# A state-space stage of four separate batches rewritten as one program with a slot for each state

## The reference, cut to what matters

```python
def _L1_attn_ref(x, W_in, conv_w, conv_b, W_x, W_dt, b_dt, A_log, D, W_out):
    xi, z = jnp.split(x @ W_in, 2, axis=-1)              # 2 x 256 channels
    xc = _silu(causal_depthwise_conv(xi, conv_w) + conv_b)   # 4 taps
    dt, Bm, Cm = jnp.split(xc @ W_x, [8, 24], axis=-1)   # 8, 16 and 16 columns
    delta = jax.nn.softplus(dt @ W_dt + b_dt)
    A = -jnp.exp(A_log)                                  # 256 x 16
    dA = jnp.exp(delta[..., None] * A)
    dBu = delta[..., None] * Bm[:, :, None, :] * xc[..., None]
    # over the 512 tokens: h = dA_t * h + dBu_t;  y_t = sum over the 16 states of h * C_t
    y = ys + xc * D
    return y * _silu(z) @ W_out
```

## Time and profile before

| | us |
|---|---|
| median of 3 runs | 3414.8 |
| lowest, highest | 3409.95, 3416.41 |
| the profiled execution's own time | 3410.95 |
| its span | 3409.0 |
| PE busy | 2794.3 (82%) |
| DVE busy | 2085.9 (61%) |
| ACT busy | 1303.8 (38%) |
| POOL busy | 913.6 (27%) |
| mean granted clock of PE | 0.907 |

### The profile page before, as it was taken

How to read it: one execution, slowest core, us unless ns; L and a number is a source line. 1 busy time by engine, 2 the same in 40 slices (tenths; PEclk the granted TensorE clock), 3 DMA queues, 4 the chain that set the end, 5 groups by cost and what they waited for, 6 DMA issues and landing times. The chain is left out here.

```text
span 3409.0 us, 40692 instructions
## 1 busy us (share of the span) xinstructions
PE 2794.3 (82%) x14561; PEld 1289.6 (38%) x14608; DVE 2085.9 (61%) x4159; ACT 1303.8 (38%) x2241; POOL 913.6 (27%) x1160
## 2 busy tenths in 40 slices
PE   4996969855565698999998999996965699698998
PEld 1332424411121353344555343443433133254555
DVE  5884861297788564566675556556667787464444
ACT  1664642233333253222121333332742466354221
POOL 2101100075467210233251545453125110110000
PEclk9997879987788798999998999997976899799999
DMA  5221300100000320121221000002200321320000
GB/s 129 36 36 48 61 22 1 50 0 0 0 1 0 64 42 2 26 51 29 63 59 43 1 1 1 1 1 38 38 0 0 54 36 25 90 45 2 1 1 13
DMA packets 45480, 94.81 MB, mean 28 GB/s; under 512 B 14168, under 2 KB 33420, under 8 KB 39520
## 3 DMA queue, kind: packets, MB, share of 16 engines
q1 hardware_dynamic: 45280, 92.22, 12.4%
HBM read 46.20 MB, written 1.38 MB: 14 GB/s over the span
## 5 line engine op out<-in xcount | busy, mean ns | idle before, releaser
L1630 POOL TENSOR_TENSOR mamba_dbu<-mamba_du,mamba_b 128x512 f32<-128x512 f32 x128 | 256.1, 2033 | 132.3 <-ACT mamba_b L1613 132.3
L1597 PE MATMUL ps<-mamba_hc,weights 128*128 128x512 f32 x256 | 164.3, 732 | 97.2 <-DVE mamba_hc L1655 96.8
L1644 DVE TENSOR_TENSOR_SCAN mamba_h<-mamba_da,mamba_dbu 128x512 f32<-128x512 f32 x128 | 211.0, 1651 | 18.3 <-ACT mamba_da L1618 18.3
L2423 DVE TENSOR_REDUCE skv_negmax<-ps 128x2 f32<-128x256 f32 (+3 forms) x128 | 105.0, 823 | 147.5 <-PE ps L2271 147.5
L534 DVE TENSOR_REDUCE L3a_negmax<-ps 128x1 f32<-128x512 f32 x256 | 162.3, 683 | 52.0 <-PE ps L294 33.7
L534 DVE TENSOR_REDUCE L0a_negmax<-ps 128x1 f32<-128x512 f32 x256 | 162.4, 683 | 50.3 <-PE ps L294 45.9
L397 ACT ACTIVATE L0a_probs<-ps 128x512 f32<-128x512 f32 x256 | 143.6, 599 | 76.6 <-PE ps L313 65.4
L397 ACT ACTIVATE L3a_probs<-ps 128x512 f32<-128x512 f32 x256 | 143.7, 599 | 74.0 <-PE ps L313 62.9
L2485 ACT ACTIVATE skv_probs<-ps 128x1024 f32<-128x1024 f32 (+3 forms) x128 | 90.2, 704 | 205.3 <-PE ps L2297 205.3
L164 POOL TENSOR_SCALAR vareps<-mv 128x4 f32<-128x4 f32 x24 | 7.6, 315 | 547.6 <-DVE mv L1271 493.4
L1801 PE MATMUL ps<-stream,xT 128*128 128x512 f32 x256 | 132.9, 640 | 10.7 <-DVE moa_v L2054 6.5
(11 more groups left out here) (625 smaller groups left out, 6661.0 us busy)
## 6 DMA issues: line engine op xcount, KB each, us to landing
moa_masks<-picked SPq DMA_DIRECT2D x32, 512.0 KB, 6.7
stream<-stream SPq DMA_DIRECT2D x32, 192.0 KB
stream<-gate_up_down_in SPq DMA_DIRECT2D x1, 4352.0 KB, 13.4
stream<-value_output_in SPq DMA_DIRECT2D x1, 4096.0 KB, 12.3
moa_gateb<-gates SPq DMA_DIRECT2D x32, 128.0 KB
stream<-ffn_in SPq DMA_DIRECT2D x1, 2888.0 KB, 9.3
L0a_qs<-L0a_qs SPq DMA_DIRECT2D x16, 128.0 KB
L0x_qs<-L0x_qs SPq DMA_DIRECT2D x16, 128.0 KB
```

Of the source, the lines that this page charges most:

```text
L1597: pe.matmul(ps[:, 4 + j, :], k.ident, hc[:, (J * n + j) % RING, :], start=n == 0, stop=n == N - 1).then_inc(s["summed"], 1)
L1630: pool.tensor_tensor(dbu[:, i % RING, :], du[:, j, :], bsb[:, n % AHEAD, :], ALU.mult).then_inc(s["dbu_ready"], 1)
L1644: dve.tensor_tensor_scan(out=hs[:, i % RING, :], data0=da[:, i % RING, :], data1=dbu[:, i % RING, :], initial=0.0, op0=ALU.mult, op1=ALU.a ...
L2423: dve.tensor_reduce(negmax[:, g % 4, qt, at:at + 2], ps[:, bank:bank + 2, 0:(qt + 1) * P], AX.X, ALU.max, negate=True).then_inc(s["maxed"], 1)
```

## The change

`mamba(k)` is called once and is one phase over the four batches. Time is counted in slots: slot S of every engine's program holds state S mod 16 of batch S div 16 (64 slots with scans, S = 0 to 63), and behind it, in the same slot, the extra steps whose turn it is. A step "at" A for batch b stands in slot 16 b + A, so the preparation of batch b, at -12 to -4, stands in slots 4 to 12 of the batch before, and the outputs, at 16 to 20, in slots 0 to 4 of the batch after. For the first batch the preparation stands in slots with no scans.

Steps of the preparation, with the slot (batch 0's count) on each engine: projection of xi, PE -12; copy, ACT -11; convolution, PE -11, as four matmuls a half with diagonal matrices of the taps, made once by POOL; silu, ACT -10; projection to step rows and B/C rows, PE -10; copies, ACT -9; step sizes, PE -9; their bias, ACT -8; split of B/C, now on POOL, -8; z, PE -8, silu of z, ACT -7; lower part, DVE -8; exp and plus one, now both on ACT, -7; rounding, DVE -6; ln, ACT -5; sum, DVE -5; delta and du, now on POOL, -4. Outputs: DVE 16, PE 17; residual and statistics, DVE 18; inverse deviation, POOL 19; rescale, DVE 19; transposes, PE 19; copy, ACT 20.

xc, sz, delta, du and bc have two buffers. The rings of scans and weighed units lie in the `stream` tile, so the load of `stream` moves behind the stage, into a block of its own. B has one PSUM bank, C three, two banks hold the sums and two serve the extra steps. After each product POOL waits for its own semaphore.

The core of the diff:

```diff
-def mamba(k, next_stream):
+def mamba(k):
...
+    TAPS, RING, C_RING, B_RING, LEAD = 4, 6, 3, 3, 2
...
+    B_BANK, C_BANK, SUM_BANK, P_BANK, Q_BANK = 0, 1, 4, 6, 7
+    XI_AT, CONV_AT, XD_AT, DT_AT, Z_AT, LOW_AT, U_AT, ERR_AT, LN_AT, DELTA_AT = -12, -11, -10, -9, -8, -8, -7, -6, -5, -4
+    Y_AT, OUT_AT, RESID_AT, XT_AT = 16, 17, 18, 19
+    FIRST, LAST = XI_AT, (BATCH - 1) * N + XT_AT + 2
...
+        hs, hc = (k.stream[:, n * RING * SEQ:(n + 1) * RING * SEQ].rearrange("p (r t) -> p r t", r=RING) for n in range(2))
...
+                def spread(i):
+                    b, n = i // N, i % N
+                    if n == 0:
+                        pe.wait_ge(s["bc_parts"], b + 1)
+                    for c, bank in ((0, B_BANK), (1, C_BANK + i % C_RING)):
+                        if c == 0 and i >= 1:
+                            pe.wait_ge(s["b_sb"], i)
+                        if c == 1 and i >= C_RING:
+                            pe.wait_ge(s["hc_ready"], J * (i - C_RING + 1))
+                        pe.matmul(ps[:, bank, :], wb(k, "stacked", ROWS3)[:, c * N + n:c * N + n + 1].to_broadcast([ROWS3, P]),
+                                  bc[:, b % 2, :], start=True, stop=True).then_inc(s["c_ready" if c else "b_ready"], 1)
...
+                def convolve(b):
+                    if b == 0:
+                        pe.wait_ge(s["taps_ready"], J * TAPS)
+                        pe.wait_ge(s["padded"], 1)
+                    for j, bank in enumerate((P_BANK, Q_BANK)):
+                        pe.wait_ge(s["xi_sb"], J * b + j + 1)
+                        take(bank, "xc_sb", J * b + j + 1)
+                        for t in range(TAPS):
+                            last = pe.matmul(ps[:, bank, :], taps[:, j, t, :], xi[:, j, t:t + SEQ], start=t == 0,
+                                             stop=t == TAPS - 1)
+                        last.then_inc(s["conv_ready"], 1)
...
+                for S in range(FIRST, LAST):
+                    if 0 <= S + LEAD < ALL:
+                        spread(S + LEAD)
+                    if 0 <= S < ALL:
+                        sums(S)
+                    if batch_at(S, OUT_AT) is not None:
+                        project_out(batch_at(S, OUT_AT))
...
+                    if batch_at(S, CONV_AT) is not None:
+                        convolve(batch_at(S, CONV_AT))
...
+                def exponential(b):
+                    act.wait_ge(s["low_ready"], b + 1)
+                    act.activation(u[:, :, :], low[:, :, :], ACT.Exp).then_inc(s["u_ready"], 1)
+                    act.wait_ge(s["u_ready"], b + 1)
+                    act.activation(w1[:, :, :], u[:, :, :], ACT.Identity, bias=1.0).then_inc(s["w1_ready"], 1)
...
+                for S in range(FIRST, LAST):
+                    if 0 <= S < ALL:
+                        copy_b(S)
+                        decay(S)
+                    if batch_at(S, CONV_AT) is not None:
+                        copy_xi(batch_at(S, CONV_AT))
+                    if batch_at(S, XD_AT) is not None:
+                        silu_conv(batch_at(S, XD_AT))
+                    if batch_at(S, DT_AT) is not None:
+                        copy_bc(batch_at(S, DT_AT))
+                    if batch_at(S, DT_AT + 1) is not None:
+                        add_dt_bias(batch_at(S, DT_AT + 1))
+                    if batch_at(S, Z_AT + 1) is not None:
+                        silu_z(batch_at(S, Z_AT + 1))
+                    if batch_at(S, U_AT) is not None:
+                        exponential(batch_at(S, U_AT))
+                    if batch_at(S, LN_AT) is not None:
+                        logarithm(batch_at(S, LN_AT))
+                    if batch_at(S, XT_AT + 1) is not None:
+                        keep_turned(k, act, s, batch_at(S, XT_AT + 1), Q_BANK)
...
+                def split_bc(b):
+                    pool.wait_ge(s["bc_sb"], b + 1)
...
+                    chain(pool.tensor_copy(out, full[:, :]))
+                    chain(pool.tensor_tensor(full[:, :], full[:, :], out, ALU.subtract))
+                    chain(pool.tensor_copy(bc[32:64, b % 2, :], full[32:64, :]))
+                    chain(pool.tensor_copy(bc[64:ROWS3, b % 2, :], full[64:ROWS3, :]))
+                    pool.tensor_tensor(bc[64:ROWS3, b % 2, :], full[64:ROWS3, :], bc[64:ROWS3, b % 2, :], ALU.subtract
+                                       ).then_inc(s["bc_parts"], 1)
...
+                def step_sizes(b):
+                    pool.wait_ge(s["v_ready"], b + 1)
...
+                    chain(pool.tensor_tensor(delta[:, b % 2], vv[:, :, :], low[:, :, :], ALU.subtract))
+                    pool.tensor_tensor(du[:, b % 2], delta[:, b % 2], xc[:, b % 2], ALU.mult).then_inc(s["du_ready"], 1)
...
+                        pool.tensor_tensor(dbu[:, m % RING, :], du[:, b % 2, j, :], bsb[:, i % B_RING, :], ALU.mult
                                            ).then_inc(s["dbu_ready"], 1)
+                        pool.wait_ge(s["dbu_ready"], m + 1)
...
-        each(lambda b: mamba(k, first(b, wstr1)))
+        mamba(k)
+        with nc.Block() as block:
+            @block.sync
+            def _(sp):
+                stream_in(sp, wstr1)
         cross_attention(k, "L1x", R8, masks=(m1q, m1k, ALU.is_equal))
```

More of the change, by code:

```diff
@@ L1600, in _, with take @@
[L1600 to L1605 removed]
+                reader = {P_BANK: None, Q_BANK: None}
+                def take(bank, sem, n):
+                    if reader[bank]:
+                        pe.wait_ge(*reader[bank])
+                    reader[bank] = (s[sem], n)
@@ new lines, in project_bc @@
+                def project_bc(b):
+                    pe.wait_ge(s["xc_sb"], J * (b + 1))
+                    take(P_BANK, "xd_sb", b + 1)
+                    for j in range(J):
+                        last = pe.matmul(ps[0:R, P_BANK, :], w_x[:, j, 0:R], xc[:, b % 2, j, :], start=j == 0, stop=j == J - 1)
+                    last.then_inc(s["xd_ready"], 1)
+                    take(Q_BANK, "bc_sb", b + 1)
+                    for j in range(J):
+                        last = pe.matmul(ps[0:ROWS3, Q_BANK, :], w_x[:, j, R:R + ROWS3], xc[:, b % 2, j, :], start=j == 0,
+                                         stop=j == J - 1)
+                    last.then_inc(s["bc_ready"], 1)
@@ new lines, in project_out, with turn_x @@
+                def project_out(b):
+                    pe.wait_ge(s["y_in"], b + 1)
+                    take(P_BANK, "y_read", b + 1)
+                    for t in range(NT):
+                        for j in range(J):
+                            last = pe.matmul(ps[:, P_BANK, t * D:(t + 1) * D], y[:, j, t * P:(t + 1) * P], w_out[:, j, :],
+                                             start=j == 0, stop=j == J - 1)
+                    last.then_inc(s["y_ready"], 1)
+                def turn_x(b):
+                    take(Q_BANK, "xT_sb", b + 1)
+                    turn_tokens(k, pe, s, b, Q_BANK)
@@ L3169, in each @@
                 stage(b)
-        def first(b, src):
-            return lambda sp: stream_in(sp, src) if b == 0 else None
         R8 = DH ** -0.5
```

372 lines of the change are left out of this document (199 added, 173 removed).

## The result

The changed kernel took 3474.7 us in the median (3473.1 to 3479.1) beside 3412.4 for the kernel before on the same chip (3408.0 to 3416.4): ratio 1.0185 [1.0167, 1.0203], 1.9% slower, +62 us. Forecast was 3430, range 3385 to 3465: the right side and, as will be shown, the right mechanism in the main, but +17 where +62 came, and 10 us outside the range. The profiled execution took 3474.5 us around a span of 3472.4.

A forecast was written before the change was run, and what follows sets the result against it. Stage: VectorE's scans taking turns with POOL's product, one per 2.15 us, bound it. 33.5 + 276.4 + 3 × (43.0 + 8.0) + 12.7 + 0.6 + 3.4 = 479.6 against 462.6, +17.0: forecast 3430 us, range 3385 to 3465.

The forecast's parts named there:

- hidden after all: Rival: ACT's copy of b is not held by the extra steps; 14.3 us a batch, 3320 us; chance 0.08.
- The slack of 2.8 us: Time b has to spare after its copy on ACT and POOL's 1.26 us, the only cover for the extra steps.
- POOL becomes the bound: Rival at POOL's queue, slots 11 and 12: own waits 10 us, delta and du 4.4 each; 22 more, 3452; chance 0.08.
- Part (c): Preparations of batches 1 to 3 inside the slots: each extra step stalls the scans, 43.0 us per batch.
- results, slots 1 to 5: Outputs of the last batch: VectorE 1.41 + 1.22, residual 1.94, rescale with transposes 2.7; 7.3 us.
- sharing a turn: Scans on VectorE after POOL's runs: two later go at 1.72 a pair, neighbouring stalls share a turn; 3.3 us off.
- part d: PE's clock: 46 passes in the seven chains, partly at half clock; 8 us a batch, bounds 0 to 19.7.
- PE cold throughout: Rival: all 46 PE passes at half clock, 19.7 us a batch; 35 more, 3465 us; chance 0.12.
- (b): First preparation, nothing beside it, convolution on PE: first scan at 33.5 us against 30.95.
- (e): Last tail 12.7 us and stage end 0.6, as now.
- (f): Load of `stream` in its own block delays L1x's start: +2.6 + 0.8 = 3.4 us.
- The two sets of tables: ACT loads separate tables for exp and ln; one set for both would cost 3 us less in all, 3427.

The follow-up runs named there:

- The two runs with the scan first: Changed kernel, POOL's second product waits for the first half's scan: states 1 to 10 and 13, 3469.2 us; then states 6 to 9 of three batches, 3461.1 us.
- The last experiment: Inverse deviation and rescale one slot later, on the version with b and decays ahead, convolution in two slots and POOL's bursts halved: 3364.2 us, ratio 0.9863.
- The filling run: Changed kernel with zero-matrix matmuls added before a state's second sum on PE, 4, or 12 in most stalling slots: 3449.8 us, ratio 1.0106.
- POOL's halved steps: Split of B/C in two slots, delta and du in two, on the version with b and decays ahead and convolution in two slots (3376.6 us): 3376.3 us.
- the run with the load alone: Kernel before, with only the load of `stream` moved behind the stage into its own block: 3416.0 us beside 3409.9, ratio 1.0010.

## Why the prediction was right in its mechanism and short in its sizes

**What held.** That ACT's in-order queue holds b and the decays of the state after next behind each extra step: moving those alone gave back 92 us, and running the steps apart, with that order kept, 91. Which slots stall: 5 to 9, 11 and 12, each one behind the slot of its step, while 10 and 13 to 15 do not, and the longest behind the convolution. The price of an unstalled slot: POOL's wait for itself costs nothing (4.29 us a slot, and 4.29 before in most slots of the same measure). Delta and du on POOL at 2.34 us each (2.45 estimated). ln and the step sizes, 2.8 and 6.9 over a normal slot (2.7 and 6.6). The rival *hidden after all* fell: the slack of 2.8 us was no match for chains of 5 to 13. Neither price of *POOL becomes the bound* came: its own waits cost nothing, and delta and du took 2.34 us each and not 4.4.

**Part (c), what failed.** A batch in the middle was to take 69.1 + 43.0 + 8.0 = 120.1 us and took 133.6, 13.5 more, three times. By slot, over 4.29 us:

```
                            forecast      measured
stalls of slots 5 to 12     39.0          51.1 (4.1 11.1 8.9 7.2 10.1 0 2.8 6.9)
results, slots 1 to 5        7.3          13.9 (2.1 1.6 4.2 4.2 1.8)
"sharing a turn"            -3.3           0
clock (part d)               8.0           in the stalls
together                    51.0          65.0
```

- *"With neighbouring stalls sharing a turn I take 3.3 off"* is the wrong step, and wrong in sign. The saving that I had in mind, a second scan that finds its product ready, does come (1.21 at 733.83), but VectorE then waits for the next chain, which starts from E in any case, and so it earns nothing. For the first scan I had charged no more than a normal turn. POOL went on to the second product, and the scan took 2.33 us in place of 1.21. Against a scan of a normal slot, 1.64, this is 0.7 us more in each of slots 5, 7, 8 and 9 and 0.1 in slot 6 (1.76): 2.9 a batch and not 3.3 less, 6.2 of the 14.0. The two runs with the scan first show the mechanism, and the scans of the second, 1.22 us each, its size.
- *The results* were charged with VectorE's and ACT's work and no wait of POOL's. The inverse deviation, ahead of the next products in POOL's queue, waits for statistics made in the same slot: 4.2 us in slot 3. The transposes then hold b on ACT in slot 4, 4.2 more, and 1.8 reach slot 5. That is 6.6 of the 14.0, read from the table of slots. The last experiment bears out the cause in slot 3, which fell to 5.75 when POOL's step stood one slot later; how much of its 12 us lies there is not shown. It is the same reading as for ACT, which I had made for one queue and not for POOL's at this place.
- *The clock*, 8 a batch: of the right size. From the timeline the scan that waits starts later after E than forecast at full clock by 1.7 us behind the convolution, 3.1 behind x/b/c (four passes 3.58 us instead of 1.88), 1.1 behind dt and 2.6 behind z: 8.5. Behind dt the forecast had the wrong end of the chain: it was to be POOL's split, at E + 6.1, and that ended at E + 4.6 (767.08); it was PE's step sizes, four passes in 3.78 us (764.50 to 768.28). So the 1.1 is less than what the clock cost there, and an error in another term hid the rest. The filling run gave back 25 us in all, 8 a batch. (The 0.7 still missing of the 14.0 is 0.4 in slots 11 and 12 and rounding.) I had it in the wrong place: the convolution does lift the clock within itself (its last eight passes run at 0.43), and x/b/c behind it runs at half again, after PE has waited for ACT's silu. The rival *PE cold throughout*, at 19.7, was above what came, as was what I had made of the Trainium skill's warning ("TensorE: Matmul & The Clock Gate", "HAM oscillation") by taking it to mean every pass; its direction, the granted clock falling from 0.80 to 0.73, agrees.

**The smaller parts.** (b) First preparation 35.3 us, not 33.5: a tap matrix on POOL takes 602 ns, not the 0.4 with its gap that an eighth of the copy had suggested, and the convolution starts at 5.8 us and not at 3.4. (e) The last tail 16.9 from the last weighing to the next block, 13.3 forecast: PE works the last eight passes of the sums in 7.21 us and the projection in 3.68, at half clock, where the kernel before did the sums at 1.98 for four. I had taken the old tail over unchanged, though the clock it ran at was one thing that the change moved. (f) L1x's start +4.3, forecast +3.4. The slots from the first scan to the last weighing took 468.2 us, forecast 276.4 + 3 × 51.0 = 429.4: 38.8 more, three times 13.5 less the 1.8 that the last batch's slot 5, with nothing of its own to prepare, doesn't lose. So 38.8 + 1.8 + 3.6 + 0.9 = 45.1 over the forecast's 17.0: 62.1, the measured 62.

**The two sets of tables.** The trace loads one for ln after exp again in each preparation, and 2.8 us for that slot is the forecast with the load in it. Whether one load could serve both was not tried.

**What stays open.** Why POOL's halved steps shorten the profiled execution and not the median, and where the 12 us of the last version lie. How clock and turn share the slots of the results, 1 to 5 of a batch, which were read for their waits alone. And why L1x starts 3.6 us later behind the moved load: the run with the load alone shows that it does, by 3.9, not which transfer it is late by.

## What to carry to other kernels

When extra steps are put between the beats of a loop, look in every engine's queue at what stands behind a step that waits, and issue the loop's own next inputs ahead of it: here the order of three lines on one engine was worth 92 us. Price each interleaved step by its chain until the loop's next input is ready, less the slack that the trace shows, and do this for each queue it passes, ACT's, POOL's and PE's. Then set it against the same steps in one piece: here they cost 36 us a batch in one piece, 65 between the scans behind the wrong queue, and 35 between them with ACT's order mended. The kernel before spends 47 on them and the best version still 30, so even well ordered most of their time was not hidden.

## What the runs showed of the hardware

- Two engines that take turns don't share them evenly after a stall: POOL's second product, issued back to back, went ahead of a scan that had been waiting for the first, and the scan took 2.33 us instead of 1.21. With the product held back the scan took 1.22; the same hold where nothing stalls cost 1.26 us a slot.
- Filling matmuls on an idle PE raised the stage's granted clock from 0.73 to 0.86 and gave 25 us; from 0.80 to 0.89, with the stalls shortened, they cost 18.6 us.
- A 128x128 float32 tensor_scalar on POOL takes 602 ns; a whole 128x1024 product of two tensors 2.34 us there when VectorE is quiet.
